# Value weights read in place, TensorE's attention heads written out, and a 53-column gather in two halves of the array

## What is computed

```python
sparsity = scores.max(axis=-1) - scores.mean(axis=-1)
_, top_idx = jax.lax.top_k(sparsity, U)                    # U = 307 of 2048, for each head
q_sel = jnp.take_along_axis(q, top_idx[..., None], axis=2)
scores_sel = jnp.einsum('bhud,bhkd->bhuk', q_sel, k) * scale
attn = jax.nn.softmax(scores_sel, axis=-1)
out_sel = jnp.einsum('bhuk,bhkd->bhud', attn, v)
out = jnp.zeros_like(q).at[bi, hi, top_idx].set(out_sel)
```

## Time and profile before

| | us |
|---|---|
| median of three runs | 1703.02 |
| the three runs | 1701.68, 1703.02, 1707.01 |
| the profiled execution, whole | 1698.9 |
| its span (first to last instruction) | 1697.2 |
| TensorE busy in the span | 1515.2 |
| VectorE busy | 1228.8 |
| ScalarE busy | 1042.7 |
| GpSimd busy | 291.7 |
| attend of b = 0, first scores of head 0 to first scores of head 15 | 137.3 |
| attend of b = 1, the same | 128.2 |

### The profile page before, as it was taken

The page is one execution under the profiler, slowest core; times in us unless marked ns, Lnnn a source line. Parts: engine busy times, 40 slices in busy tenths (PEclk is TensorE's granted clock), DMA queues, the critical chain, the costliest instruction groups (busy, mean ns, idle before and its releaser), DMA issues.

```text
span 1697.2 us, 29054 instructions
## 1 busy us (share of the span) xinstructions
PE 1515.2 (89%) x8702; PEld 845.3 (50%) x8702; DVE 1228.8 (72%) x2916; ACT 1042.7 (61%) x1401; POOL 291.7 (17%) x354
## 2 busy tenths in 40 slices
PE   6899999998769989999998869989899999989999
PEld 3442222223334432222222644544598987469988
DVE  5479999998667639999999877866755552665511
ACT  4578888887545658888887436673333373334364
POOL 2340000003524335000000214441111100111100
PEclk9999999999989999999999989999999999999999
DMA  4761111130421121111112101111034402004410
GB/s 155 226 185 37 37 48 45 37 93 30 150 65 48 44 64 38 37 37 51 42 37 84 60 29 48 49 32 62 13 118 143 137 25 77 0 25 158 158 47 31
DMA packets 93325, 119.13 MB, mean 70 GB/s; under 512 B 22754, under 2 KB 78658, under 8 KB 92740
## 3 DMA queue, kind: packets, MB, share of 16 engines
q1 hardware_dynamic: 90180, 117.60, 22.8%
q0 software_dynamic: 3072, 0.66, 0.4%
HBM read 93.41 MB, written 24.78 MB: 70 GB/s over the span
## 4 chain that ended last, share of the span: by engine, by line
PE 44%; DVE 32%; issue 13%; DMA 4%; ACT 4%; POOL 1%; SPq 1%; PEld 0%; DVEq 0%; ACTq 0%; PEldq 0%; POOLq 0%
DVE work_area L1188 24%; PE psum L2044 6%; PE psum L1982 6%; PE psum L1849 5%; PE psum L1838 4%; PE psum L1925 4%; PE psum L1826 3%; PE psum L1993 3%; PE psum L2002 3%; DVE big_area L1188 2%; PE psum L1671 2%; DMA work_area<-heads_out 2%; PE psum L2034 2%; PE psum L1696 1%; ACT work_area L827 1%
## 5 line engine op out<-in xcount | busy, mean ns | idle before, releaser
L1188 DVE CUSTOM_DVE_ANT_0 work_area<-psum,work_area 128x1024 f32<-128x1024 f32 x512 | 589.2, 1220 | 8.1 <-PE psum L1732 4.3
L809 ACT ACTIVATE work_area<-psum 128x1024 f32<-128x1024 f32 x512 | 510.6, 1026 | 76.4 <-DVE big_area L1188 31.0
L1732 PE MATMUL psum<-work_area 96*128 96x512 bf16 x1024 | 309.4, 384 | 48.3 <-DVE big_area L1188 7.3
L1722 PE MATMUL psum<-work_area 96*128 96x512 bf16 x1024 | 305.4, 380 | 7.4 <-ACT work_area L809 1.7
L827 ACT ACTIVATE work_area<-psum 128x614 f32<-128x614 f32 x256 | 163.7, 681 | 101.8 <-PE psum L1838 93.5
L1732 PEld LDWEIGHTS psum<-work_area 96*128 96x128 bf16 x1024 | 63.4, 97 | 266.7 <-DVE big_area L1188 250.4
L1722 PEld LDWEIGHTS psum<-work_area 96*128 96x128 bf16 x1024 | 88.8, 98 | 153.0 <-ACT work_area L809 59.1
L663 POOL DMA_INDIRECT heads_out<-work_area x96 | 99.0, 1031 | 168.5 <-DVE work_area L1352 147.5
L1323 DVE TENSOR_SCALAR big_area<-iota,rank 128x308 bf16<-128x308 f16 x512 | 121.7, 312 | 0.0
L1982 PE MATMUL psum<-work_area,xn 128*128 128x128 f32 x1024 | 117.3, 275 | 0.0
L1925 PE MATMUL psum<-slots_T,work_area 128*128 128x512 f32 x256 | 117.1, 601 | 0.0
(11 more groups left out here) (256 smaller groups left out, 1996.2 us busy)
## 6 DMA issues: line engine op xcount, KB each, us to landing
work_area<-in_L_ffn_w_dram SPq DMA_DIRECT2D x32, 1024.0 KB, 5.2
work_area<-k_parts SPq DMA_DIRECT2D x192, 64.2 KB
work_area<-q_parts SPq DMA_DIRECT2D x192, 64.0 KB
k_parts<-work_area SPq DMA_DIRECT2D x24, 384.0 KB, 3.3
q_parts<-work_area SPq DMA_DIRECT2D x16, 384.0 KB, 2.9
big_area<-q_parts SPq DMA_DIRECT2D x16, 384.0 KB, 5.4
work_area<-k_parts SPq DMA_DIRECT2D x32, 192.0 KB
x_res<-in_L_attn_x_dram SPq DMA_DIRECT2D x8, 512.0 KB, 4.8
```

The lines of the kernel that those rows point to most:

```text
L809: s.activation(SC[:, t % 4], PS[:, 2 * (n % 2):2 * (n % 2) + 2].rearrange("p a n -> p (a n)"), ACT.Relu).then_inc(relu_done, 1)
L1188: v.tensor_tensor_reduce(SC[:, t % 4], PS[:, 4 + 2 * (t % 2):6 + 2 * (t % 2)].rearrange("p a n -> p (a n)"), SC[:, t % 4], 1.0, -3.0e38, A ...
L1722: last = mm(PS[:, 2 * (n % 2) + k], QS1[par][0:TERMS, t * P:(t + 1) * P], KS[par][0:TERMS, k * 512:(k + 1) * 512], start=True, stop=True)
L1732: last = mm(PS[:, 4 + 2 * (t % 2) + k], QS1[par][0:TERMS, t * P:(t + 1) * P], KS[par][0:TERMS, K1 + k * 512:K1 + (k + 1) * 512], start=Tru ...
```

## The change

- `Vh` and GpSimd's `build` are gone. `values` takes `V[:, kt, head]` (17 columns) as weights and writes 17 of the 32 rows of each group. TensorE waits once for `v_done` and `v_ones` ahead of the stage.
- SK holds each part once: 48 columns of parts, 3 of shift, 2 of index, 64 with padding. VectorE's `build` is two copies in place of seven. GpSimd sets SK to zero in `pads`.
- `gather` writes tiles of even number to PSUM rows 0 to 63 and those of odd number to rows 64 to 127 of bank 4, each a matmul with 64 weight columns. The two halves are partial sums of the same rows.
- ScalarE's new `take_gathered` copies all 128 rows to GQ (bf16). TensorE's new `spread` multiplies by `spread_rows`, a matrix of zeros and ones, which adds the halves and lays out the 101 rows as before. `take_queries` then copies them to QS as it did.
- The gather's cuts are 6, 6 and 4 tiles (before 5, 6 and 5). `take_gathered` stands between exponentials 4 and 5. `spread` stands between `rows` and `turn`.
- TensorE's 16 heads are all written out.
- GpSimd builds `spread_rows` at the start of the kernel.

```diff
@@ constants of the kernel and areas
+    HALF_ROWS = 64
+    PARTS = 3 * DH
-        Vh = a.take([2, NT, 32])
-        SK = a.take([2, NT, TERMS + 6], BF16)
+        SK = a.take([2, NT, HALF_ROWS], BF16)
+        GQ = a.take([UP], BF16)
@@ GpSimd
+            g.memset(spread_rows[:], 0.0).then_inc(pstep, 1)
+            pool.wait_ge(pstep, ps.next())
+            for half in range(2):
+                for at, part in enumerate((0, 0, 0, 1, 1, 2)):
+                    cols = spread_rows[:, at * DH:(at + 1) * DH]
+                    g.affine_select(out=cols, in_=cols, compare_op=ALU.not_equal, fill=1.0, base=-(half * HALF_ROWS + part * DH), pattern=[[-1, DH]], channel_multiplier=1)
...
             def pads(b):
 
-                g.memset(Vh, 0.0).then_inc(pads_ready, 1)
                 g.memset(OS, 1.0).then_inc(pads_ready, 1)
                 pool.wait_ge(rank_ready, b + 1)
                 pool.wait_ge(nm_ready, b + 1)
+                g.memset(SK, 0.0)
                 for k in range(2):
                     last = g.memset(K2S[k], 1.0)
                 last.then_inc(pads_ready, 1)
-                pool.wait_ge(pads_ready, 3 * (b + 1))
...
-                build(0, 0, 0)
-                build(0, 1, 1)
-                with pool.Fori(0, PAIRS - 1) as i:
+                with pool.Fori(0, PAIRS) as i:
                     for par in range(2):
-                        build(i, par, par + 2)
                         scatter(i, par, par)
@@ ScalarE
+                def take_gathered(i, n):
+
+                    act.wait_ge(gathered, b * H + i * 2 + (n + 3))
+                    s.activation(GQ[:, 0:U], PS[:, 4, 0:U], ACT.Identity).then_inc(gq_ready, 1)
+
                 def take_queries(i, par, n):
 
-                    act.wait_ge(gathered, b * H + i * 2 + (n + 3))
+                    act.wait_ge(spread_ready, b * H + i * 2 + (n + 1))
...
                 def act_head(i, par, more):
-                    exps(i, par, range(0, 7))
+                    exps(i, par, range(0, 5))
+                    if more:
+                        take_gathered(i, par + 1)
+                    exps(i, par, range(5, 7))
                     if more:
                         take_queries(i, 1 - par, par + 1)
                     exps(i, par, range(7, 8))
@@ VectorE
-                    for at, r in enumerate((0, 0, 0, 1, 1, 2)):
-                        v.tensor_copy(SK[:, par, :, at * DH:(at + 1) * DH], QN[:, :, r, bass.ds(hd, DH)])
-                    v.tensor_copy(SK[:, par, :, TERMS:TERMS + 3], NM[:, :, bass.ds(h, 1)].rearrange("p t o r -> p t (o r)")).then_inc(sk_ready, 1)
+                    v.tensor_copy(SK[:, par, :, 0:PARTS].rearrange("p t (r d) -> p t r d", r=3), QN[:, :, :, bass.ds(hd, DH)])
+                    v.tensor_copy(SK[:, par, :, PARTS:PARTS + 3], NM[:, :, bass.ds(h, 1)].rearrange("p t o r -> p t (o r)")).then_inc(sk_ready, 1)
@@ TensorE
-                        last = mm(PS[0:TERMS + 5, 4, 0:U], SK[:, n % 2, t, 0:TERMS + 5], OH[:, n % 2, t, 0:U], start=(t == 0), stop=(t == NT - 1), skip_group_check=True)
+                        at = t % 2 * HALF_ROWS
+                        last = mm(PS[at:at + HALF_ROWS, 4, 0:U], SK[:, n % 2, t], OH[:, n % 2, t, 0:U], start=(t < 2), stop=(t >= NT - 2), skip_group_check=True)
...
+                def spread(i, n):
+
+                    pe.wait_ge(gq_ready, b * H + i * 2 + (n + 1))
+                    mm(PS[0:TERMS + 5, 4, 0:U], spread_rows[:, 0:TERMS + 5], GQ[:, 0:U], start=True, stop=True).then_inc(spread_ready, 1)
...
-                        last = mm(PS[32 * q:32 * q + 32, 6 - n % 2, 0:U], Vh[:, n % 2, kt], PX[:, kt // 2 % 4, kt % 2, 0:U], start=(kt < 4), stop=(kt >= NT - 4), skip_group_check=True)
+                        last = mm(PS[32 * q:32 * q + DH + 1, 6 - n % 2, 0:U], V[:, kt, i * 2 + n], PX[:, kt // 2 % 4, kt % 2, 0:U], start=(kt < 4), stop=(kt >= NT - 4), skip_group_check=True)
...
-                CUTS = (0, 5, 11, NT)
+                CUTS = (0, 6, 12, NT)
...
                         if k4 == 2:
                             rows(i, n)
+                            if later > 0:
+                                spread(i, n + 1)
                             if not first:
                                 turn(i, n - 1)
...
-                pe_head(0, 0, True, 2)
-                pe_head(0, 1, False, 2)
-                with pe.Fori(1, PAIRS - 1) as i:
-                    for n in range(2):
-                        pe_head(i, n, False, 2)
-                pe_head(PAIRS - 1, 0, False, 1)
-                pe_head(PAIRS - 1, 1, False, 0)
+                for h in range(H):
+                    pe_head(h // 2, h % 2, h == 0, min(2, H - 1 - h))
                 turn(PAIRS - 1, 1)
```

31 lines of the change are left out of this document (15 added, 16 removed).

## The result

The changed kernel takes 1736.78 us (median of four runs, 1733.86 to 1738.26), the kernel before 1704.51 us beside it: a ratio of 1.0192 with a 95% interval of 1.0163 to 1.0220. It is slower, as forecast, but by 32 us where the forecast had 8.5, and above the upper end of the range (1727).

The account below looks back on a forecast made before the run. TensorE's own 7.96 us was taken as a head's floor, with stalls of 1.16 and 0.50 us. Terms -0.5 + 7.3 + 0.8 + 0.9 = 8.5 us on 1703.0 gave 1711.5 us, range 1695 to 1727.

Parts of the forecast that it names:

- ScalarE's order: Chain through ScalarE's two copies in attend: a head takes 8.9 us, 7.36 of TensorE work and 1.5 of waits.
- the prediction's two sums: Attend from first scores of head 0 to head 15: 136.8 us for b = 0, 135.5 for b = 1.
- The two tables loaded behind exponential 7: Once in b = 1 ScalarE changes its tables twice, delaying exponential 0 and score pair 2: 2.0 us more.
- The old stall falls into them: Stall ahead of exponential 4 falls into the new waits; half a microsecond late, but exponential 5 waits for `gathered` anyway.
- a late release: Rival in attend: TensorE's late release moves onto the gather's end, `gathered` 0.5 us late, +14 us, 1725 us; chance 0.10.
- The `build` drew the stall out: GpSimd's `build` behind the third indirect DMA drew out the stall in b = 0; gone with the change.
- Gather in halves: Paired half matmuls overlap on TensorE: six tiles 0.55 us, four tiles 0.40, saving 0.73 us a head.
- each weight load would show: In no-overlap rival (0.10, 1735 us): weight loads of the halves not hidden, about 0.85 us a head, similar result.
- Keys: Key load of 9.1 us, needed 10.3 us after issue, is hidden; 3.3 us of wait before head 15, b = 0.
- The rival's floor of 8.2 us: Rival: copies hidden, key loads hold a head at 8.2 us, 1692 us in all; chance 0.13.
- Start of attend: Third memset of 1.77 us delays the key load ahead of attend: +0.8 us in b = 0, +0.9 in b = 1.

Follow-up runs that it names:

- after_four: Changed kernel with its three indirect DMAs a head spaced, four buffers of IDX and ON, GpSimd's and VectorE's heads written out: 1706.8 us, ratio 1.0025.
- filler: Changed kernel with 12 matmuls whose result nobody reads put ahead of score pair 6: 1729.6 us, ratio 1.0179.
- v_direct: Kernel before with values' weights straight from V, no `build`, and TensorE's heads written out, gather as before: 1694.8 us, ratio 0.9971.
- order_no_scatter: Changed kernel with take_gathered behind exponential 5, take_queries behind exponential 7, and the 96 indirect DMAs left out: 1676.4 us, ratio 0.9890.
- early_four: Changed kernel with 8+8 gather tiles ending behind values 0, copies and spread earlier, indirect DMAs spaced, four IDX/ON buffers: 1674.2 us, ratio 0.9804.

## Why the prediction was wrong, point by point

- **ScalarE's order**: right. The chain gave 8.9 us a head; heads without a stall take 8.81. With the signals in time (after_four) the two stages take 135.8 + 135.4 = 271.2 us; the prediction's two sums are 136.8 + 135.5 = 272.3. That they agree so closely is in part luck: 30 heads at 8.81 are 2.7 us less, and the first heads, at the lower clock, 1.8 us more, which stood in no term. The two tables loaded behind exponential 7 cost 11.12 - 8.81 = 2.3 us (forecast 2.0).
- **"The old stall falls into them"**: this step failed. The forecast let the indirect DMAs fall near score pair 4 again and took the stall as covered by the wait for `gathered`. They fall there, but the signals are late until 0.6 to 0.8 us behind the third DMA, exponential 4 starts 1.5 us late and everything behind it moves by 0.84 us a head. The prediction had named a late release, but took it for something of `onehot` and `build`, and asked only when the DMA ends. As a rival it was priced at 0.5 us and a chance of 0.10, to decide only if the third DMA ended later than 1.8 us into the count: in head 6 it ends at 547.29 - 545.98 = 1.31, and the signals still come 0.7 us behind it. The two stages in filler (full clock, late signals) take 288.6 us, in after_four 271.2: 17 us.
- **The clock** was in no step. The gaps of the new order and the stall together put TensorE to its lower level for some 3 us in every second head of b = 0 and some of b = 1: 300.6 - 288.6 = 12 us. The gaps that the forecast itself wrote down (0.9, 0.3 and 0.3 us) do not do it alone: in after_four, which has them without the stall, the clock stays at 1.00 from 487.8 to 617.5. So this loss came in with the failed step. In the kernel before, with shorter gaps, it stayed at 1.00 from 483.6 to 620.1. Not so the first heads: they cost 10.14 and 9.94 us where 8.81 was due, 2.5 us together, and still 9.68 and 9.73 in after_four. The Trainium skill (TensorE: Matmul & The Clock Gate, A second HAM failure mode: psum-queue depth-cycling) tells of a kernel whose clock swings because TensorE idles briefly and often between groups of matmuls; the rows above agree. I had not weighed it.
- **"The `build` drew the stall out"**: wrong. v_direct has none and keeps 9.05 us; VectorE's `onehot` is not needed either, since the heads that end the stage have no `onehot` beside them and stall alike: in head 14 VectorE does nothing from 626.24 on, and exponential 4 again waits until 0.73 us behind the third DMA.

```profile
625.76 0.48 DVE L1347 COPY work_area<-psum 128x307 f32<-128x307 f32 x1 [0.84 <-PE psum L1857]
628.06 1.07 POOL L664 DMA_INDIRECT heads_out<-work_area  x1 [0.30 <-issue]
...
629.86 0.68 ACT L828 ACTIVATE work_area<-psum 128x614 f32<-128x614 f32 x1 [1.99 <-PE psum L1848]
```

- **Gather in halves**: right. Six gather matmuls run from 543.68 to the next scores at 544.20, 0.52 us (forecast 0.55), four in 0.38 (0.40). That each weight load would show, which the prediction had drawn as a rival from the Trainium skill (TensorE: Matmul & The Clock Gate, Part 3), the trace does not bear out.
- **Keys**: hidden between heads, as forecast. The 3.3 us of wait ahead of head 15 of b = 0 are only 0.29 us here, since the heads are longer; at the forecast pace they come (2.95 us in after_four). The rival's floor of 8.2 us was too high: order_no_scatter runs at 7.60 us with one head held up by keys, and they show regularly only in early_four.
- **Start of attend**: the mechanism right, the size not to be told. The third memset took 1.80 us (forecast 1.77), and the keys do bind: the last signal of their load comes at 483.19, the copy of the queries, which the row below names as the releaser, was done at 482.53, and the first scores start at 483.28. The forecast had 485.1, counted from the 470.71 of the trace before; here the ranks are ready and the memsets begin at 469.10, 1.6 us earlier, and the load from 474.74 on takes 8.45 us, not 9.1. In the traces of the kernels with the halves the first scores of b = 0 start anywhere from 483.2 to 485.3, before 484.39, so 0.8 us more or less cannot be read from one of them.

```profile
469.10 1.80 POOL L651 MEMSET work_area<- 128x2048 bf16 x1 [2.50 <-DVE rank L1317]
...
474.74 4.48 SPq L462 DMA_DIRECT2D work_area<-k_parts  x6
...
478.79 2.27 PE L1831 MATMUL psum<-big_area,work_area 128*64 128x307 bf16 x16 [12.92 <-DVE big_area L1328]
...
483.28 1.19 PE L1848 MATMUL psum<-work_area 99*128 99x307 bf16 x4 [1.21 <-ACT work_area L820]
```

Together: 35 us in attend where the sum had 6.8. Of the 28 that were missing, late signals make 17 and the clock that falls with them 12; the sum itself was 1 us too high. The whole follows, since outside attend the two profiled executions differ by 0.4 us.

## What to carry to other kernels

Shorter work on one engine is worth nothing where the chain goes through another engine's strict order: put the copy where that engine idles anyway (8.81 to 6.88 us a head here). Price a stall that you see in the profile where the changed order will put it, find its cause before you call it covered, and count what a new gap does to the clock of the engine that waits. Take the suspected work out once, as in the run without scatter: it gives the bound of what mending can bring.

## What the runs showed of the hardware

- Signals of TensorE to ScalarE come late while GpSimd issues indirect DMAs 1.29 us apart: the wait ends 0.6 to 0.8 us behind the third in b = 0. The ends of matmuls are modelled in the profile, so it shows that their completion is told late, while TensorE's next instructions start on time; ScalarE's own signals are not late. With one a head, or with three some 2 to 4 us apart, hardly any are late. It cost 18 us in the kernel before and was the larger of the two new losses in attend. Why TensorE's signals suffer was not found; nor why b = 1 of the kernel before loses less (8.46 against 9.12 us a head) with the same spacing, its exponential 4 starting 0.2 us ahead of the third DMA's end in most heads. The Trainium skill (SBUF — State Buffer, Who interferes with whom) tells of GpSimd and VectorE blocking each other at their shared port, and says that TensorE and ScalarE never wait for anyone. No run here shows the first as the cause, since VectorE does nothing beside the stall of head 14; the second is said of the memory's ports, and these late signals are not covered by it.
- Behind two gaps of 1.03 and 0.46 us TensorE's granted clock fell to 0.53 for 3.3 us; with 0.76 us of unused matmuls in the larger gap it stayed at 1.00 from 489.8 to 629.7. The heads between, with the same gaps, kept the full clock without fillers.
